# A selective-scan layer with a routed expert layer: Softplus by one function, the input projection in three f32r passes, the shared expert added into the last scaled bank, the skip term moved to GpSimd, another split of VectorE and GpSimd work

## What is computed

```python
xz = layernorm(x) @ W_in + b_in            # 128 -> 512
x_proj, z = split(xz);  u = silu(x_proj)   # 256 channels each
B, C = split(u @ W_xproj + b_xproj)        # 16 states each
dt = softplus(u @ W_dt + b_dt)
h_t = h_{t-1} * exp(dt_t * A) + (dt_t * u_t) * B_t     # for 256 channels x 16 states
y_t = sum_s h_t * C_t + D * u_t
x = x + (y * silu(z)) @ W_out + b_out

xt = layernorm(x)
scores = softmax(xt @ gate_w.T);  combine = the scores of the top 2 of (scores + bias), else 0
x = x + sum_e mlp(xt; w1[e], w2[e], w3[e]) * combine[:, e] + mlp(xt; sw1, sw2, sw3)   # 8 experts, 1 shared
# mlp(x) = (silu(x @ w1.T) * (x @ w3.T)) @ w2.T, 256 inner features
```

## Time and profile before

| | |
|---|---|
| median of 3 runs | 1234.91 us |
| the profiled execution | 1235.3 us, span 1233.3 us |
| busy share of the span | PE 94%, DVE 92%, ACT 92%, POOL 85% |
| ACT_TABLE_LOADs | 227, 1283 ns each |
| DMA | 153.67 MB, mean 125 GB/s |

### The profile page before, as it was taken

How to read it: one execution, slowest core, us unless ns; L and a number is a source line. 1 busy time by engine, 2 the same in 40 slices (tenths; PEclk the granted TensorE clock), 3 DMA queues, 4 the chain that set the end, 5 groups by cost and what they waited for, 6 DMA issues and landing times.

```text
span 1233.3 us, 21816 instructions
## 1 busy us (share of the span) xinstructions
PE 1157.0 (94%) x7200; PEld 946.7 (77%) x7200; DVE 1130.1 (92%) x1833; ACT 1138.8 (92%) x1982; POOL 1042.8 (85%) x534
## 2 busy tenths in 40 slices
PE   5466899999999999999999999999999999999998
PEld 3344576878888787878888787887878788888887
DVE  3788899999999999999999999999999999999754
ACT  6666999999999999999999999999999999989854
POOL 2999999999989999998999998999899899987300
PEclk8677999999999999999999999999999999999999
DMA  8333152506034160613325060433407043330000
GB/s 297 155 141 142 73 215 77 222 10 268 34 148 155 52 242 9 240 61 148 154 80 214 10 272 30 155 147 120 182 8 286 9 163 131 164 129 10 10 9 10
DMA packets 48016, 153.67 MB, mean 125 GB/s; under 512 B 4512, under 2 KB 29472, under 8 KB 31392
## 3 DMA queue, kind: packets, MB, share of 16 engines
q1 hardware_dynamic: 47904, 152.28, 31.9%
HBM read 147.03 MB, written 5.24 MB: 123 GB/s over the span
## 4 chain that ended last, share of the span: by engine, by line
ACT 50%; PE 26%; issue 10%; POOL 8%; DVE 4%; SPq 1%; DMA 1%; DVEq 0%; ACTq 0%; POOLq 0%
ACT da L661 13%; PE h L1021 13%; ACT L661 8%; ACT mixed L704 7%; ACT silu L697 6%; PE mixed L990 6%; PE y_acc L1003 5%; POOL dbu L754 4%; ACT L697 4%; DVE hc L856 3%; POOL hc L764 2%; ACT xn L677 1%; ACT xt L611 1%; ACT L642 1%; ACT lin L636 1%
## 5 line engine op out<-in xcount | busy, mean ns | idle before, releaser
L754 POOL TENSOR_TENSOR dbu<-w_s,b_all 128x1024 f32<-128x1024 f32 x256 | 604.3, 2383 | 2.1 <-DMA c_all<-bc_rows 2.1
L764 POOL TENSOR_TENSOR hc<-hc,c_all 128x1024 f32<-128x1024 f32 x128 | 304.6, 2380 | 92.0 <-DVE hc L856 91.6
L661 ACT ACTIVATE da<-dt_s,a_neg 128x512 f32<-128x512 f32 x512 | 342.1, 689 | 30.5 <-DVE hc L856 16.0
L1003 PE MATMUL y_acc<-ident,hc 128*128 128x128 f32 x2048 | 290.9, 279 | 35.8 <-POOL hc L764 25.0
L856 DVE TENSOR_TENSOR_SCAN hc<-da,dbu 128x512 f32<-128x512 f32 x256 | 302.2, 1211 | 18.6 <-ACT da L661 14.7
L856 DVE TENSOR_TENSOR_SCAN da<-da,dbu 128x512 f32<-128x512 f32 x256 | 308.1, 1216 | 10.4 <-POOL dbu L754 6.0
L1003 PEld LDWEIGHTS y_acc<-ident,hc 128*128 128x128 f32 x2048 | 246.5, 144 | 87.5 <-POOL hc L764 35.7
L990 PE MATMUL mixed<-w_s,g 128*128 128x128 f32 x2304 | 284.0, 276 | 4.6 <-DVE acc L906 1.8
L990 PEld LDWEIGHTS mixed<-w_s,g 128*128 128x128 f32 x2304 | 272.6, 192 | 20.0 <-DVE g L898 10.2
L1021 PE MATMUL h<-x_hi,w_hi 128*128 128x512 f32 x576 | 273.4, 475 | 9.6 <-ACT silu L697 6.2
L1021 PE MATMUL h<-x_hi,w_lo 128*128 128x512 f32 x576 | 228.2, 396 | 0.0
...
## 6 DMA issues: line engine op xcount, KB each, us to landing
b_all<-bc_rows SPq DMA_DIRECT2D x64, 1024.0 KB, 6.4
c_all<-bc_rows SPq DMA_DIRECT2D x64, 1024.0 KB, 8.8
...
```

What stands on the lines that cost most here:

```text
L661: act.activation(da[a % DA_SLOTS][:, :], dt_s[:, c, :], ACT.Exp, scale=a_neg[:, a:a + 1]).then_inc(decay_made, 1)
L754: pool.tensor_tensor(dbu[:, at:at + AT_ONCE, :], w_s[:, c, None, :].broadcast_to([P, AT_ONCE, T]), b_all[:, s:s + AT_ONCE, :], ALU.mult).t ...
L764: pool.tensor_tensor(pair, pair, c_all[:, s:s + 2, :], ALU.mult).then_inc(c_by_pool, 1)
L1003: last = pe.matmul(y_acc[:, b, :], hc[:, a % HC_SLOTS, b * P:(b + 1) * P], ident[:, :], is_transpose=True, start=False, stop=(a % NS == NS ...
```

## The change

dt becomes one function, Softplus, written into two alternating slots; `softe`, `softl` and GpSimd's `dt` are gone:

```diff
-                    act.activation(soft[:, a, :], tile[:, :], ACT.Abs, bias=bias).then_inc(magnitudes, 1)
-                    act.activation(lin[:, a, :], tile[:, :], ACT.Relu, bias=bias).then_inc(freed, 1)
-                elif what == "softe":
-                    act.activation(soft[:, :, :], soft[:, :, :], ACT.Exp, scale=-1.0).then_inc(soft_steps, 1)
-                elif what == "softl":
-                    act.activation(soft[:, :, :], soft[:, :, :], ACT.Ln, bias=1.0).then_inc(soft_steps, 1)
+                    if m > 1:
+                        act.wait_ge(decay_made, STEPS * (m - 2) + NS * (a + 1))
+                        act.wait_ge(w_made, NC * (m - 2) + a + 1)
+                    act.activation(dt_s[:, m % DT_SLOTS, a, :], tile[:, :], ACT.Softplus,
+                                   bias=bdt_s[:, a:a + 1]).then_inc(freed, 1)
...
-                    pool.tensor_tensor(dt_s[:, a, :], soft[:, a, :], lin[:, a, :], ALU.add).then_inc(dt_made, 1)
```

The projection works on a split of the weights and of the normalised input (the raw weights are loaded into `b_all`'s first slot, before anything else but x); `x_lo` is new on VectorE, and `h1`, `h3` use the same helper:

```diff
+            act.activation(win_hi[:, :], win_raw, ACT.Copy).then_inc(win_hi_made, 1)
...
+                    act.activation(xn_hi[:, :], tile[:, :], ACT.Copy).then_inc(xn_hi_made, 1)
...
+                    dve.tensor_tensor(xn_lo[:, :], tile[:, :], xn_hi[:, :].bitcast(F32), ALU.subtract).then_inc(freed, 1)
...
+            def three_passes(dst, w_hi, w_lo, x_hi, x_lo):
+
+                for i, (w, xx) in enumerate(((w_hi, x_hi), (w_hi, x_lo), (w_lo, x_hi))):
+                    last = pe.matmul(dst[:, :], w, xx[:, :], start=(i == 0), stop=(i == 2))
+                return last
...
-                        last = pe.matmul(tile[:, :], win_s[:, col:col + P], xnT[:, :], start=True, stop=True)
+                        last = three_passes(tile, win_hi[:, col:col + P], win_lo[:, col:col + P], xn_hi, xn_lo)
```

The shared expert is now number 8. Its `eo` matmuls add into the bank of expert 7 after `sc.7` has scaled it, so that there are eight `comb` instead of nine:

```diff
+                elif what == "shared":
+
+                    pe.wait_ge(g_made, UNITS * (m + 1))
+                    pe.wait_ge(scaled, E * (m + 1))
+                    expert_out(mixed_tile("eo", E - 1, m), E, False).then_inc(shared_added, 1)
...
+                    if what == "comb" and a == E - 1:
+                        dve.wait_ge(shared_added, m + 1)
```

From sequence 2 on GpSimd adds the skip term to step 0 and step 16's product, and the eight transposes of L999 go:

```diff
+                elif what == "add":
+
+                    first_step = NS * a
+                    pool.wait_ge(skip_made, NC * (m + 1))
+                    pool.wait_ge(*c_count(first_step, m))
+                    at = hc[:, first_step % HC_SLOTS, :]
+                    pool.tensor_tensor(at, at, skip[:, a, :], ALU.add).then_inc(added, 1)
...
+                    if a % NS == 0 and m >= SKIP_BY_PE:
+                        pe.wait_ge(added, NC * (m - SKIP_BY_PE) + c + 1)
```

The split of the C products now depends on the sequence, and VectorE makes `norm1` and both `w` of sequence 0:

```diff
-BY_DVE = [0,1,4,5,8,9,12,13,16,17,20,21,24,25,28,29]
+BY_DVE = [0,1,4,5,8,9,12,13,16,17,20,21,24,25]
+
+BY_DVE_FIRST = [
+                [0, 1, 2, 3, 4, 5, 8, 9, 12, 13, 16, 17, 20, 21, 24, 25, 28, 29, 30, 31],
+                [0, 1, 4, 5, 8, 9, 12, 13, 16, 17, 20, 21, 24, 25, 28, 29, 30, 31],
+                [0, 1, 4, 5, 8, 9, 12, 13, 16, 17, 20, 21, 24, 25, 28, 29],
+]
```

The layer norm's shift is one VectorE instruction in place of four, `x2T` shares memory with `xn2`, and TensorE's warm-up matmuls go from 16 to 28:

```diff
-WARM_UP = 4
+WARM_UP = 7
...
-                    for b in range(NB):
-                        last = dve.tensor_scalar(sh[:, b:b + 1], mom[:, b, 0:1], r[:, b:b + 1], -1.0,
-                                                 ALU.mult, ALU.mult)
+                    dve.scalar_tensor_tensor(out=sh[:, :], in0=mom[:, :, 0], scalar=-1.0, in1=r[:, :],
+                                             op0=ALU.mult, op1=ALU.mult).then_inc(made, 1)
```

More of the change, by code:

```diff
@@ L39, with by_dve, by_pool @@
 MIXED_BANKS, H_BANKS = 2, 3
+DT_SLOTS = 2
 SILU_SLOTS, G_SLOTS = 6, 3
-BY_DVE = [0,1,4,5,8,9,12,13,16,17,20,21,24,25,28,29]
-BY_POOL = [a for a in range(STEPS) if a not in BY_DVE]
-POOL_PAIRS = BY_POOL[::2]
-assert all(a % 2 == 0 and a + 1 in BY_POOL for a in POOL_PAIRS)
+BY_DVE = [0,1,4,5,8,9,12,13,16,17,20,21,24,25]
+BY_DVE_FIRST = [
[3 rows of a table added]
+]
+SKIP_BY_PE = 2
+def by_dve(m):
+    return BY_DVE_FIRST[m] if m < len(BY_DVE_FIRST) else BY_DVE
+def by_pool(m):
+    return [a for a in range(STEPS) if a not in by_dve(m)]
@@ L49 @@
+assert all(b == a + 1 and a % 2 == 0 for m in range(SEQS) for a, b in zip(by_pool(m)[::2], by_pool(m)[1::2]))
 ORDER = {
     "pe": """
[L51 to L54, removed]
@@ L58 @@
     """,
     "act": """
[L60 to L64, removed]
@@ L68 @@
+        decay.30-1 silu.13-3 silu.14-3 silu.15-3 silu.16-3 silu.17-3 decay.31-1 decay.0 norm2.0-2 decay.1
+        sc.6-3 skip.0 xhi.0-2 splitc.0-2 decay.2 ycopy.1-1 decay.3 sc.7-3 decay.4 decay.5 rexp.0-2 silu.0-2
+        silu.1-2 silu.2-2 decay.6 decay.7 decay.8 decay.9 silu.3-2 silu.4-2 silu.5-2 sc.0-2 silu.6-2
+        silu.7-2 silu.8-2 decay.10 decay.11 decay.12 decay.13 norm1.0+1 sc.1-2 decay.14
     """,
     "dve": """
-        g.0-2 mul.29-1 g.1-2 scan.30-1 scan.31-1 rank.0-2 g.2-2 rank.1-2 scan.0 rank.2-2 comb.0-2 rank.3-2
@@ L78 @@
+        mul.12 mul.13 comb.1-2 scan.14 scan.15 comb.2-2 projc.0-1 scan.16 scan.17 mul.16 g.6-2 g.7-2
+        mom2.0-1 mul.17 scan.18 x_lo.0+1 scan.19 g.8-2 comb.3-2 scan.20 scan.21 g.9-2 mul.20 mul.21 scan.22
+        scan.23 scan.24 scan.25 mul.24 mul.25 g.10-2 agg2.0-1 g.11-2 scan.26 scan.27 nb2.0-1 scan.28 g.12-2
+        mom1.0+2 comb.4-2 scan.29
     """,
     "pool": """
-        dbu.15 rs1.0+2 hcp.26 dbu.0+1 hcp.30 dbu.1+1 dbu.2+1 dbu.3+1 hcp.2+1 resb.0 dbu.4+1 dbu.5+1 hcp.6+1
-        dbu.6+1 dbu.7+1 dt.1+1 w.1+1 rs2.0 hcp.10+1 dbu.8+1 dbu.9+1 hcp.14+1 dbu.10+1 hcp.18+1 dbu.11+1
@@ L204 @@
+        h3.13 h1.16 h3.14 h3.15 eo.6 h1.17 h3.16 eo.7 h3.17 shared.0
     """,
     "act": """
[L206 to L209 removed]
@@ L820, in task @@
                                       ALU.subtract).then_inc(weights_split, 1)
+                elif what == "norm1":
+                    dve.wait_ge(rstd1_made, m + 1)
+                    for b in range(NB):
+                        last = dve.tensor_scalar(xt[:, b, :], xt[:, b, :], moments[:, b, 0:1], rstd[:, b:b + 1],
+                                                 ALU.subtract, ALU.mult)
+                    last.then_inc(norm1_made, 1)
+                elif what == "w":
+                    dve.wait_ge(*taken("dl", a, m))
+                    dve.wait_ge(*taken("xp", a, m))
+                    dve.tensor_tensor(w_s[:, a, :], dt_s[:, m % DT_SLOTS, a, :], u[:, a, :], ALU.mult).then_inc(w_made, 1)
                 elif what in ("mom1", "mom2"):
```

492 lines of the change are left out of this document (256 added, 236 removed).

## The result

The changed kernel takes 1238.08 us (median of 20 runs), the kernel before 1235.03 beside it (20 runs): a ratio of 1.0027, 95% interval 1.0016 to 1.0038. (One of the changed kernel's 20 runs was in a slower state, 2284 us, and is not in the ratio.) I had forecast a clear gain, 1194 us. The profiled execution has a span of 1235.7 us against 1233.3.

The account below looks back on a forecast made before the run. It took TensorE, ScalarE and VectorE as full at once in the middle. Start -15.5, middle -24 and end -1.3 made -40.8 us from 1235.3, so 1194 us, with 1180 to 1212 as the range.

Parts of the forecast that it names:

- ScalarE: Each middle sequence: Softplus for branches, Exp and Ln, and two fewer table loads; busy time -5.6 us, 70.2 to 64.6.
- its slack covers waits: Middle sequences: ScalarE's new slack should cover waits like those of scans for decays; period taken as 69.0 us.
- VectorE: Each middle sequence: fewer multiplications, one comb and shift instructions less, x_lo added; busy time -1.9 us, 69.6 to 67.7.
- TensorE: Each middle sequence: cheaper input projections and no skip-term transposes; busy time -1.6 us, 70.5 to 68.9.
- The projection: TensorE, each middle sequence: three f32r passes at 0.69 for one f32 product at 0.86 us, four times, saving 0.7.
- the skip transposes: TensorE, each middle sequence: the eight transposes of the skip term go, saving 0.9 us.
- GpSimd: Each middle sequence: dt goes, one pair of C products and two adds come; busy time +2.3 us, 65.2 to 67.5.
- The first rival: Middle: GpSimd becomes the bound and keeps its waits, period 73.3 us, total about 1247 us; chance 0.06.
- The period: Twelve middle sequences: 71.0 falls to 69.0 us each, -24 us in all; bounds 68.0 and 70.2.
- The third rival: Middle gives nothing: late decays and three h banks keep the period at 71.0 us, total 1218 us; chance 0.06.
- The start: Sequences 0 to 2: earlier first dbu and less GpSimd work; -15.5 us, bounds -4 and -20.
- The end: After the last first decay: less TensorE work, about 0.9 us of matmuls open; -1.3 us, between -4 and +3.

Follow-up runs that it names:

- a1: The changed kernel with the layer norm's shift by four tensor_scalar instructions again instead of one; 1225.70 us, 0.9926 of the kernel before.
- a6: a1 with the experts' silu replaced by a Copy, which takes its table loads away too; 1219.76 us.
- c2: a1 with the input projection as one f32 product for each half, as in the kernel before; 1230.88 us.
- c1: a1 with the skip term by TensorE's transposes in every sequence and GpSimd's two adds gone; 1233.43 us.
- a4: The changed kernel with GpSimd's pairs of C products made for the first of the two steps only; 1227.21 us.
- d2: The kernel before with steps 28 and 29 multiplied by C on GpSimd instead of VectorE in every sequence; 1299.86 us, ratio 1.0525.
- a5: a1 with two of three passes in h, half of each g and half of each GpSimd pair of C products; 1193.96 us.
- c5: a1 with the old split of C products between VectorE and GpSimd in sequences 0 and 1 too; 1232.88 us.
- a2: The changed kernel with two passes instead of three in h1 and h3, on TensorE; 1226.43 us.

## Why the prediction was wrong

Forecast were -40.8 us, and the spans differ by +2.4. Of the 43.2 between, 32.4 lie in the twelve sequences from the fourth on (-24 forecast, 860.5 for 852.1 measured, +8.4), 10.1 in the start (-15.5 forecast, -5.4 measured) and 0.7 behind. The shift is worth 12.4 of it by a1, which is still 31 us above the forecast.

- **ScalarE** (-5.6): measured -4.8, with twelve loads and a Softplus as long as a decay, as priced. The step that failed is the next one, that its slack covers waits: it became waits for the two decay banks, and relieving it by 7 more us (a6) gave 0.4 a sequence.
- **VectorE** (-1.9): here the working failed. "Two groups of four shifts become two single ones, 8 x 0.12 to 2 x 0.12": a gain of 0.73 was a loss of 0.5, the difference of a1 and the changed kernel ((413.69 - 410.49) / 6), since in the middle one takes 0.4 and the other 1.3 (0.96 on average over the whole). The other terms were right: with the shift by four VectorE falls by 1.2, which is 1.9 less the 0.7. I had the rule and a row for it, and set it aside with "in the middle no VectorE instruction of size has both inputs in SBUF". What counted was not the size of the VectorE instruction but what was left of GpSimd's, and GpSimd is busy 95% of the middle.
- **TensorE** (-1.6): measured -0.3, and -0.6 with the shift by four. The projection saves 0.25, not 0.7, the skip transposes 0.6, not 0.9 (c2, c1). Both terms have one misreading: the earlier trace rows shows 0.32 from the first pass at 603.00 to the next at 603.32, and 0.36 for the four transposes before it; I took 0.23 for the pass and gave the rest, 0.45 in all, to the transposes. My distance of 0.5 between TensorE's busy time and the period held: 70.5 and 71.0 before, 69.9 and 70.3 in a1.
- **GpSimd** (+2.3): right, 67.4. The first rival named its full queue; in the new order it wasn't what cost (a4: 9.7 us less gave 0.6), on the old order it was (d2). That rival's 1247 is the nearest to the time measured, for a cause that isn't the one here.
- **The period** (69.0): measured 71.0. With the shift by four it is 70.3. The other 1.3: I took one limit, TensorE's at 69.4 or VectorE's at 69.1, and let ScalarE's slack lower it; they are 69.8 and 69.7, and the period lies 0.5 above both. That this comes of their being so close is my reading, not tried. The third rival had the number, 71.0, for the middle, but its reason, ScalarE's late decays, is not the cause: with ScalarE's work as it is and the others' cut, 68.8 is reached (a5).
- **The start** (-15.5): the first `dbu` at 28.33 was nearly as forecast (27 to 28). Sequence 0 took 63.5 us where 56 was needed for the 83 forecast (83 less 26.6); VectorE was busy 58.08 where I had 51. The three `w_lo` beside GpSimd's instructions took 2.70, 1.79 and 1.75 instead of 0.69, which is the same wait for GpSimd and 4.2 of the 7 us, and c5 shows that VectorE's sum is not all of it. The first decay of sequence 3 came at 223.1, where I had said near 213.
- **The end** (-1.3): measured -0.6. But the last full sequence, which I counted as one of the twelve at -2.0, gave +10.4, the costliest single stretch. I never compared what the two orders leave to it. The order tables hold these counts; how long the stretch would take they don't say, as a2 shows.
